# One plan for four layers: norms, routing and experts of a sandwich kernel by batch row

## The chip, the cores and the metric

The kernel runs on one core of a Trainium2 chip, in one launch. The metric is device microseconds of that core, the median of three runs. TensorE is PE, VectorE DVE, ScalarE ACT, GpSimd POOL; SyncE (SP) issues every DMA of the part that matters here.

## What is computed

`x` is (2, 1024, 128): two batch rows. A first block (layernorm, 16-head attention with cluster affinities, MLP) is added to it and is untouched by the change. The second block is `x + layernorm(ffn(layernorm(x)))`, all in float32, where `ffn` is four layers of

```python
h = _rms(x, ln1_w[l])
h = _attention(h, wq[l], wk[l], wv[l], wo[l], cos, sin, causal_bias)
x = jnp.clip(res + h, -100.0, 100.0)
...
h = _rms(x, ln2_w[l])
h = _moe(h, wr[l], wg[l], wu[l], wd[l])
x = jnp.clip(res + h, -100.0, 100.0)
```

with 16 query heads on 4 key heads of 64, causal, rotary; and 8 experts of width 256, of which the two likeliest count, `out += comb[e] * ((silu(x @ wg[e]) * (x @ wu[e])) @ wd[e])`. Every expert is computed for every token.

## The kernel before

Precision comes from split operands: each float32 matmul operand is a high part (a cast copy) and a low part (the difference), and a product is three matmuls, high by high, low by high, high by low. The high parts are made by ACT, the low ones by DVE or POOL.

A layer is one pass of a loop (`Fori`) that all five engines run. Four stages follow one another.

1. **Norm** (`norm_vector`, `norm_scalar`, `norm_tensor`, n5): 16 tiles of 128 tokens, both batch rows in one go: squares, sums, square root, scaling (L533), transposes (L584), then `xh` and `xl`.
2. **Attention** (`attention_order`, table `LAYER`): a "head" n is one key head with its four query heads, for one batch row: row n % 2, so heads 6 and 7 are the last of row 0 and row 1. Per head: projections P (three per half of the row), rotary products on DVE (L1483, L1484), halves swapped by DMA into `rbp`, sum on POOL (L771), high parts H on ACT, low parts L on POOL (L776) and K on DVE (L1489), copies Q by DMA into the stacks, maxima M (PE L1166, DVE L1501), turned into a row J and sent to the stack by DMA; then per step of 128 keys S (scores, L1184), exponential on ACT (L905), probabilities summed on POOL (L764), V (L1196), and per tile D (denominator L1208, reciprocal L1459) and O (L1215, L1472). The engines' order is computed ahead of time by `planned` from a cost in ns for each step and is fixed; head n+1 is prepared while head n attends, the first head while nothing does. W are the value projections of both rows.
3. **Norm n6 and routing**: again both rows at once; router matmuls (L1248, L1249), 19 dependent DVE steps (`route`, L1525 to L1545), then the weights of the experts turned into `combT` (8 partitions by 2048 tokens).
4. **Experts**: two experts per loop pass, both batch rows for one expert: a unit is 512 tokens by 128 of the hidden width. `up2` makes gate and up (six matmuls), ACT applies Silu (L933), DVE multiplies, POOL makes the low part (L788), `down2` adds three matmuls into one of four banks. The routing weight of a token reaches all partitions by a matmul of `sel` with `combT` into `psC`, and DVE multiplies by it:

```python
vec.tensor_tensor(hid[:, i % 4, :], gate[:, i % 2, :], psG[:, (2 * i + 1) % 3, :], ALU.mult).then_inc(s_hf, 1)
...
vec.tensor_tensor(hid[:, i % 4, :], hid[:, i % 4, :], psC, ALU.mult).then_inc(s_hc, 1)
```

Expert weights are loaded by SP into `est`, copied high on ACT (`split_high`, L879) and made low on POOL (`ready`, L744), once per expert.

## Time and profile before

| | |
|---|---|
| median of three runs | 3838.05 us (3833.82 to 3839.37) |
| profiled execution, its own time | 3821.54 us |
| its span | 3819.2 us |
| mean granted TensorE clock | 0.924 |
| busy: PE, DVE, ACT, POOL | 3384.5, 2759.9, 1672.0, 2031.2 us |
| share of the chain that ended last: PE, DVE, issue, POOL | 66%, 14%, 9%, 6% |

Durations below are of the profiled execution. A busy PE is not a PE at its peak: matmuls overlap, so the spacing of their starts says more than their durations.

### The profile page before, as it was taken

The page shows a single profiled execution, that of the slowest core. Times are in us where ns is not written, and L with a number is a line of the kernel's source. Part 1 is how long each engine was busy: PE and PEld are TensorE (multiplying, and loading weights), DVE is VectorE, ACT ScalarE, POOL GpSimd, SP SyncE. Part 2 cuts the span into 40 slices and gives each one's busy share as a digit, 9 for nine tenths or more (in the row PEclk, how much of TensorE's full clock was granted, in tenths as well). Part 3 has the DMA queues.
Part 4 walks back from the last instruction along what each step waited for, and adds up shares of the span by engine and source line. Part 5 has one row for each costly group of instructions (what it writes and reads, how often), then busy time and mean ns, then how long its engine had stood idle before and what let it go on. Part 6 is the DMA issues. An engine that isn't in the chain of part 4 may idle for free.

```text
span 3819.2 us, 65097 instructions
## 1 busy us (share of the span) xinstructions
PE 3384.5 (89%) x18456; PEld 2247.9 (59%) x18456; DVE 2759.9 (72%) x4711; ACT 1672.0 (44%) x3133; POOL 2031.2 (53%) x1615
## 2 busy tenths in 40 slices
PE   5899999739999979699999795999998869999897
PEld 2455555426666657466666574666656646666575
DVE  7877787358788756588886566887856668888566
ACT  3266666423444345334443453344334524444344
POOL 2100000036878646368787463778774638787654
PEclk9589899959999989799999897999998979999999
DMA  0000000043324101333331013333310134232001
GB/s 15 1 1 2 2 1 1 17 104 75 85 68 91 28 6 39 76 74 81 76 76 26 9 36 80 84 67 84 70 24 13 37 83 92 61 90 68 9 17 30
DMA packets 113175, 181.33 MB, mean 47 GB/s; under 512 B 26560, under 2 KB 54080, under 8 KB 112576
## 3 DMA queue, kind: packets, MB, share of 16 engines
q1 hardware_dynamic: 112832, 177.26, 20.1%
q8 instruction: 154, 2.52, 0.3%
q14 instruction: 189, 1.55, 0.1%
HBM read 23.45 MB, written 2.10 MB: 7 GB/s over the span
## 4 chain that ended last, share of the span: by engine, by line
PE 66%; DVE 14%; issue 9%; POOL 6%; ACT 3%; DMA 1%; SPq 1%; POOLq 0%; DVEq 0%; ACTq 0%
PE psO L1196 11%; PE psA L1184 7%; PE psA L1166 6%; PE psA L1185 6%; DVE rden L1459 4%; PE psO L1052 3%; PE psA L1040 3%; PE psA L1029 3%; PE psA L1272 3%; POOL xw L764 3%; PE psA L1274 3%; PE psA L1273 3%; PE psO L1215 2%; PE psO L1208 2%; PE psA L1169 1%
## 5 line engine op out<-in xcount | busy, mean ns | idle before, releaser
L905 ACT ACTIVATE prob<-psA 128x512 f32<-128x512 f32 x1152 | 658.4, 597 | 1083.7 <-PE psA L1185 321.9
L764 POOL TENSOR_TENSOR xw<-xw,prob 128x512 f32<-128x512 f32 x672 | 882.4, 1313 | 180.1 <-ACT prob L905 100.0
L1501 DVE TENSOR_REDUCE mxp<-psA 128x1 f32<-128x512 f32 (+3 forms) x1024 | 542.5, 583 | 129.4 <-PE psA L1166 118.8
L1184 PE MATMUL psA<-qs,ks 128*128 128x512 f32 x1152 | 539.0, 468 | 26.3 <-DMA qs<-mrow 21.9
L1459 DVE RECIPROCAL rden<-psO 128x256 f32<-128x256 f32 x256 | 449.2, 1755 | 153.5 <-PE psO L1208 116.9
L1166 PE MATMUL psA<-ks,qs 128*128 128x512 f32 (+3 forms) x1536 | 496.2, 399 | 50.7 <-DMA qs<-normed 49.0
L788 POOL TENSOR_TENSOR hidl<-hid,hidh 128x512 fp32r<-128x512 f32 x256 | 330.8, 1298 | 284.7 <-ACT hidh L943 284.5
L764 POOL TENSOR_TENSOR xw<-prob 128x512 f32<-128x512 f32 x224 | 291.7, 1302 | 353.3 <-ACT prob L905 265.7
L1185 PE MATMUL psA<-qs,ks 128*128 128x512 f32 x1152 | 455.4, 395 | 0.0
L1166 PEld LDWEIGHTS psA<-ks,qs 128*128 128x128 f32 x1536 | 299.9, 202 | 101.9 <-issue 53.7
L1400 DVE TENSOR_REDUCE mxp<-psA 128x1 f32<-128x512 f32 x512 | 315.2, 682 | 40.4 <-PE psA L1029 40.4
L853 ACT ACTIVATE pr<-psA 128x512 f32<-128x512 f32 x512 | 271.8, 602 | 125.6 <-PE psA L1040 124.3
L771 POOL TENSOR_TENSOR ra<-ra,rbp 128x512 f32<-128x512 f32 x192 | 240.1, 1281 | 145.9 <-DMA rbp<-rb 145.9
L1558 DVE TENSOR_TENSOR hid<-gate,psA 128x512 f32<-128x512 f32 x256 | 176.0, 687 | 189.6 <-ACT gate L933 189.5
L1184 PEld LDWEIGHTS psA<-qs,ks 128*128 128x128 f32 x1152 | 222.2, 193 | 144.9 <-issue 101.4
L1196 PE MATMUL psO<-prob,vv 128*64 128x256 f32 x2304 | 291.5, 385 | 3.1 <-ACT prob L905 2.9
L1196 PE MATMUL psO<-prob,outer 128*64 128x256 f32 x2304 | 291.4, 386 | 0.6
L933 ACT ACTIVATE gate<-psA 128x512 f32<-128x512 f32 x256 | 153.0, 598 | 251.1 <-PE psA L1274 250.9
L714 POOL COPY outer<-qkv 128x256 f32 x8 | 3.2, 402 | 465.1 <-PE psO L1052 465.1
L1501 DVE TENSOR_REDUCE mxq<-psA 128x1 f32<-128x384 f32 (+3 forms) x512 | 220.2, 483 | 35.8 <-PE psA L1169 31.2
L1169 PE MATMUL psA<-maskq,identb 128*128 128x128 bf16 x1024 | 241.9, 237 | 0.0
L1185 PEld LDWEIGHTS psA<-qs,ks 128*128 128x128 f32 x1152 | 220.4, 191 | 17.5
(244 smaller groups left out, 6454.3 us busy)
## 6 DMA issues: line engine op xcount, KB each, us to landing
qs<-normed SPq DMA_DIRECT2D x384, 256.0 KB, 4.9
rbp<-rb SPq DMA_DIRECT2D x256, 192.0 KB, 3.5
est<-in_L_ffn_wg SPq DMA_DIRECT2D x32, 128.0 KB, 2.1
est<-in_L_ffn_wu SPq DMA_DIRECT2D x32, 128.0 KB, 2.1
est<-in_L_ffn_wd SPq DMA_DIRECT2D x64, 64.0 KB, 1.9
wst<-in_L_ffn_wq SPq DMA_DIRECT2D x4, 512.0 KB, 4.4
wos<-in_L_ffn_wo SPq DMA_DIRECT2D x64, 32.0 KB, 2.1
outer_kept<-outer SPq DMA_DIRECT2D x1, 1024.0 KB, 6.4
```

The lines of the kernel that those rows point to most:

```text
L764: g.tensor_tensor(psum_k[:, t % 2, :], before, prob[:, i % 4, :], ALU.add).then_inc(s_su, 1 if kt > 1 else 2 + (t == 1))
L788: g.tensor_tensor(hidl[:, i % 4, :], hid[:, i % 4, :], hidh[:, i % 4, :], ALU.subtract).then_inc(s_hl, 1)
L853: act(pr1[:, j % 2, h, :], psS1[:, n % 3, :], ACT.Exp).then_inc(s_ex1, 1)
L905: act(prob[:, k % 4, :], psS[:, k % 2, :], ACT.Exp, scale=float(HD) ** -0.5).then_inc(s_ex, 1)
L1166: ins = mm(bank[:, 0:k1 - k0], qs1[b][:, c, h, t % TPC * P:(t % TPC + 1) * P], ks[b][:, 0, k0:k1], start=True, stop=not diagonal)
L1169: ins = mm(bank[:, k1 - k0 - P:k1 - k0], identb[:, :], maskq[:, :], start=False, stop=True)
L1184: mm(psS[:, i % 2, :], ks[b][:, 0, tile], qs1[b][:, c, :, qs], start=True, stop=False)
L1185: ins = mm(psS[:, i % 2, :], ks[b][:, 1, tile], qs2[b][:, c, :, qs], start=False, stop=(kt < t))
L1196: ins = mm(psO[t % 2][q * HD:(q + 1) * HD, 0:256], vv[b][:, kt, g * HD:(g + 1) * HD], prob[:, i % 4, q * 256:(q + 1) * 256], start=(kt == ...
L1400: vec.tensor_reduce(mxp1[:, m // 2, m % 2:m % 2 + 1], psM1[:, (m + 1) % 3, :], AX.X, ALU.max).then_inc(s_mr1, 1)
L1459: vec.reciprocal(rden[:, :], psO[t % 2][:, 256:512]).then_inc(s_rd, 1)
L1501: vec.tensor_reduce(dst, ring[SLOT["M", n, t, m] % N_RING][:, 0:k1 - k0], AX.X, ALU.max).then_inc(s_mr, 1)
```

## The change

The loop over layers goes: `network_order` plans the 4 layers as one table `NETWORK`, and each engine walks through it once, unrolled. In it

- norms are per batch row (steps Nc, Ns, Nv, Nd, Nm, T, Nh, Nl; q numbers them, four a layer), and so are routing (G, Ga, Ge, Gb, Gt, Gc) and experts: the order of units is row, expert, half of the row, half of the width, and each expert's weights are loaded and split once for each row (`Ew`, `Eh`, `El`), from two `est`;
- head 0's preparation in the next layer (`EARLY`) uses banks 6 and 7, which row 1's experts don't, and may run beside them; so may row 0's norm. Gate and up have banks 0 to 3, row 0's down sums 6 and 7, row 1's 4 and 5;
- routing weights are copied to `wrow`, written to DRAM (`Gd`), and come back by a DMA per 512 tokens that repeats them on all partitions (`B`, tile `spread`, three buffers); DVE multiplies by that tile. `combT`, `sel`, `psC`, `zeros` and their matmuls are gone. The hidden tile stays in `gate` (three buffers), and `hidh` and `hidl` have three;
- the gain of a norm is applied by the scale of ACT's copy and inside DVE's low part; the query's low part is written straight into its stack.

```diff
-def ring_order():
-    order = [("P", 0, c, u) for c in range(NCH) for u in range(3)]
-    for n in range(HEADS):
-        for c in range(NCH):
-            order += [("M", n, t, m) for t in range(c * TPC, (c + 1) * TPC) for m in range(len(max_pieces(t)))]
-            order += [("J", n, c)]
-            if n + 1 < HEADS:
-                order += [("P", n + 1, c, u) for u in range(3)]
-    return order
...
+EARLY = projections(0, 0) + [("W", j) for j in range(TPB // 2)] + projections(0, 1) + chunk_maxima(0, 0) + [("J", 0, 0)]
+MAIN = chunk_maxima(0, 1) + [("J", 0, 1)] + projections(1, 0) + [("W", j) for j in range(TPB // 2, TPB)] + projections(1, 1)
+for head in range(1, HEADS):
+    for half in range(NCH):
+        MAIN += chunk_maxima(head, half) + [("J", head, half)] + (projections(head + 1, half) if head + 1 < HEADS else [])
+N_PAIR = MAIN.index(("J", 0, 1)) + 1
+BANK = {item: 6 + i % 2 for i, item in enumerate(EARLY)}
+BANK.update({item: 2 + i % 2 if i < N_PAIR else (4, 5, 2, 3)[(i - N_PAIR) % 4] for i, item in enumerate(MAIN)})
+BEFORE, seen_in = {}, {}
+for item in EARLY + MAIN:
...
+UNITS = B * E * 4
+EXPERTS = L * B * E
+NORMS = 4 * L
...
+def unit(n):
+    return n // UNITS, n // (UNITS // B) % B, n // 4 % E, n // 2 % 2, n % 2
...
-def attention_order():
...
+def network_order():
...
+    def norm(q, b, ready, old, banks):
+        for h in range(2):
+            stage("scalar", ("Ns", q, h), 560, ready, ("tensor", ("T", q - 1, 1)) if q else None)
+        stage("vector", ("Nv", q), 1560, ("scalar", ("Ns", q, 1)))
+        stage("scalar", ("Nd", q), 1500, ("vector", ("Nv", q)))
+        stage("vector", ("Nm", q), 1700, ("scalar", ("Nd", q)))
+        for h in range(2):
+            stage("tensor", ("T", q, h), 500, ("vector", ("Nm", q)), *banks[h])
+            stage("scalar", ("Nh", q, h), 650, ("tensor", ("T", q, h)), *old)
...
+    def expert_weights(w):
+        l = w // (B * E)
+        stage("sync", ("Ew", w), 2000, ("gpsimd", ("El", w - 2)) if w > 1 else None,
+              ("tensor", ("S", l, HEADS - 1, TPB - 1, TPB - 1)) if w % (B * E) == 1 else None)
+        stage("land", ("Ew", w), 2500, ("sync", ("Ew", w)))
+        stage("scalar", ("Eh", w), 950, ("land", ("Ew", w)), ("tensor", ("Y", 4 * w - 5)) if w > 1 else None,
+              ("tensor", ("S", l, HEADS - 1, TPB - 1, TPB - 1)) if w % (B * E) == 1 else None)
...
+    def expert_unit(n):
+        l, b, e, c, f = unit(n)
+        w, k, g = n // 4, n // 2, B * l + b
+        start = [("scalar", ("S", l, HEADS - 1, TPB - 1, TPB - 1)), ("scalar", ("J", l, HEADS - 1, 1))] if n % UNITS < 2 else \
+            [("scalar", ("Si", n - 2)), ("vector", ("Hf", n - 2))]
+        if f == 0:
+            stage("sync", ("B", k), 650, ("land", ("Gd", g)), ("vector", ("Hw", 2 * k - 5)) if k > 2 else None)
+            stage("land", ("B", k), 2500, ("sync", ("B", k)))
+        stage("tensor", ("U", n), 1300, ("gpsimd", ("El", w)), ("vector", ("Nl", 4 * l + 2 + b, c)), *start)
+        stage("scalar", ("Si", n), 610, ("tensor", ("U", n)), ("gpsimd", ("Hl", n - 3)) if n > 2 else None)
+        stage("vector", ("Hf", n), 700, ("scalar", ("Si", n)))
+        stage("vector", ("Hw", n), 700, ("vector", ("Hf", n)), ("land", ("B", k)))
+        stage("scalar", ("Hh", n), 630, ("vector", ("Hw", n)), ("tensor", ("Y", n - 3)) if n > 2 else None)
+        stage("gpsimd", ("Hl", n), 1320, ("scalar", ("Hh", n)))
+        bank = [("vector", ("O", l, HEADS - 1, TPB - 1))] if b == 0 else [("scalar", ("Gc", g, 1))]
+        stage("tensor", ("Y", n), 650, ("gpsimd", ("Hl", n)), *(bank if e == 0 and f == 0 else []))
+    for l in range(L):
+        if l == 0:
...
+        for w in range(l * B * E, (l + 1) * B * E):
+            expert_weights(w)
+        if l + 1 < L:
+            weights(l + 1)
+        for n in range(l * UNITS, (l + 1) * UNITS):
+            expert_unit(n)
...
+NETWORK = network_order()
...
+        qs2_1, hidh, hidl, est1 = over("qs2_1", [P, NCH, GQ, CH], F32R, ("hidh", [P, 3, 512], F32R), ("hidl", [P, 3, 512], F32R), ("est1", [P, WE], F32))
...
+        est = [sb("est0", [P, WE], where=second), est1]
+        spread = sb("spread", [P, 3, 512], where=second)
...
+        qs1_1, eh1, el1, gate = over("qs1_1", [P, NCH, GQ, CH], F32R, ("eh1", [P, WE], F32R), ("el1", [P, WE], F32R), ("gate", [P, 3, 512], F32))
...
+        routing = nc.dram_tensor("routing_weights", (L * B, E, SEQ), F32, kind="Internal").ap()
...
+                elif what == "Gd":
+                    g = i[0]
+                    sp.wait_ge(s_cth, 2 * g + 2)
+                    sp.dma_start(routing[g], wrow[:, :]).then_inc(s_gd, 16)
+                elif what == "B":
+                    k = i[0]
+                    l, b, e, c, _ = unit(2 * k)
+                    sp.wait_ge(s_gd, 16 * (B * l + b + 1))
+                    if k > 2:
+                        sp.wait_ge(s_hw, 2 * (k - 2))
+                    sp.dma_start(spread[:, k % 3, :], routing[B * l + b, e:e + 1, c * CH:(c + 1) * CH].broadcast_to([P, CH])).then_inc(s_wb[k % 3], 16)
+                else:
...
-                nothing = zeros[:, :].unsqueeze(1).broadcast_to([P, NT, P])
-                g.tensor_tensor(combT[:, :].rearrange("p (a n) -> p a n", a=NT), nothing, nothing, ALU.add).then_inc(s_cz, 1)
...
+                    g_.wait_ge(s_hi, 4 * u + w + 1)
+                    if l and n == 1:
+                        g_.wait_ge(s_yd, UNITS * l)
+                        if w == 0:
+                            g.memset(qs2[1][0:HD, c, 0:GQ:2, :].bitcast(F32), 0.0).then_inc(s_qz, 1)
...
+                    g.tensor_tensor(hidl[:, n % 3, :], gate[:, n % 3, :], hidh[:, n % 3, :], ALU.subtract).then_inc(s_hl, 1)
...
+                    act(xh[:, b * SEQ + h * CH:b * SEQ + (h + 1) * CH], turned_bank(q, h), ACT.Copy,
+                        scale=fcol[:, w * L + l:w * L + l + 1]).then_inc(s_nh, 1)
...
-                def weights(ep, i):
-                    pair, i = l * (E // 2) + ep + i // (2 * N_UNIT), i % (2 * N_UNIT)
-                    ee, c = i // N_UNIT, i // 2 % 4
-                    if c == 0:
-                        t_.wait_ge(s_se, pair * 2 + ee + 1)
-                    t_.wait_ge(s_hc, pair * 2 * N_UNIT + i + 1)
-                    mm(psC, sel[:, ee, :], combT[:, c * 512:(c + 1) * 512], start=True, stop=True).then_inc(s_cb, 1)
...
-                for c in range(4):
-                    for n in range(4):
-                        ins = nc.tensor.transpose(acc[c][0:E, n * P:(n + 1) * P], comb[:, 4 * c + n, :], ident[:, :])
...
+                if n % UNITS < 2:
+                    t_.wait_ge(s_ex, (l + 1) * N_ATTN + 4)
+                    t_.wait_ge(s_mc, (l + 1) * HEADS * NCH)
+                else:
+                    t_.wait_ge(s_si, n - 1)
+                    t_.wait_ge(s_hf, n - 1)
+                expand(banks[2 * n % 4], n // 4, f * P, cs)
+                expand(banks[(2 * n + 1) % 4], n // 4, FF + f * P, cs).then_inc(s_gu, 1)
...
-                        vec.tensor_tensor(hid[:, i % 4, :], gate[:, i % 2, :], psG[:, (2 * i + 1) % 3, :], ALU.mult).then_inc(s_hf, 1)
-                        v.wait_ge(s_hf, n + 3)
-                        v.wait_ge(s_cb, (l * (E // 2) + ep) * N_UNIT + i // 2 + 1)
-                        vec.tensor_tensor(hid[:, i % 4, :], hid[:, i % 4, :], psC, ALU.mult).then_inc(s_hc, 1)
...
+                elif what == "Hf":
+                    n = i[0]
+                    v.wait_ge(s_si, n + 1)
+                    vec.tensor_tensor(gate[:, n % 3, :], gate[:, n % 3, :], banks[(2 * n + 1) % 4], ALU.mult).then_inc(s_hf, 1)
+                elif what == "Hw":
+                    n = i[0]
+                    v.wait_ge(s_hf, n + 1)
+                    v.wait_ge(s_wb[n // 2 % 3], 16 * (n // 6 + 1))
+                    vec.tensor_tensor(gate[:, n % 3, :], gate[:, n % 3, :], spread[:, n // 2 % 3, :], ALU.mult).then_inc(s_hw, 1)
...
```

DVE inside the experts. Before, a unit is two multiplications, the second with the weights in `psA`:

```order
L1558 TENSOR_TENSOR hid<-gate,psA 128x512
L1560 ISA
L1561 TENSOR_TENSOR hid<-hid,psA 128x512
L1555 REGISTER_ALU
L1556 REGISTER_ALU
L1558 TENSOR_TENSOR hid<-gate,psA 128x512
L1561 TENSOR_TENSOR hid<-hid,psA 128x512
```

Now, in the first layer's row 0 (`rt` and `r` are row 1's routing, `spread` the routing weights of row 0):

```order
L1758 TENSOR_TENSOR gate<-gate,psA 128x512
L1763 TENSOR_TENSOR gate<-gate,spread 128x512
L1640 TENSOR_REDUCE rt<-psA 128x64
L1642 TENSOR_REDUCE r<-rt 128x8
L1644 TENSOR_TENSOR rt<-rt,r 128x64
L1684 TENSOR_TENSOR wal<-wst,wah 128x1536
L1685 TENSOR_TENSOR wvl<-wvst,wvh 128x256
L1686 TENSOR_TENSOR wrp<-wrs,wrp 128x8
L1646 TENSOR_REDUCE r<-rt 128x8
L1648 TENSOR_TENSOR rt<-rt,r 128x64
L1650 TENSOR_TENSOR rt<-rt,order 128x64
L1652 TENSOR_REDUCE r<-rt 128x8
```

The second multiplication reads two tiles in SBUF, and the steps of row 1's routing, of which the rest follow without a break, stand between two units.

PE at the end of the experts. Before, the last units of a layer end it, and the next layer begins with the norm's transposes:

```order
L1288 REGISTER_ALU
L1289 MATMUL psA<-hidh,eh 128x512
L1290 MATMUL psA<-hidh,el 128x512
L1291 MATMUL psA<-hidl,eh 128x512
L1325 MATMUL psA<-ident,hid 128x128 x16
```

Now, among the last units of row 1 (`hidh`, `eh`: down and up of the first layer's experts; `ks`, `qs_0`: maxima of the second layer's head 0, `maskq` their mask):

```order
L1324 MATMUL psO<-ks,qs_0 128x128
L1327 MATMUL psO<-maskq,identb 128x128
L1324 MATMUL psO<-ks,qs_0 128x128
L1327 MATMUL psO<-maskq,identb 128x128
L1414 MATMUL psA<-hidh,eh 128x512
L1415 MATMUL psA<-hidh,el 128x512
L1416 MATMUL psA<-hidl,eh 128x512
L1324 MATMUL psO<-ks,qs_0 128x128
L1327 MATMUL psO<-maskq,identb 128x128
L1386 MATMUL psA<-xh,eh 128x512
L1387 MATMUL psA<-xl,eh 128x512
```

The maxima of the next layer's head 0, which stood behind the loop's end, now stand between units; its norm and projections stand further ahead among them in the same way.

## Rows read from the trace of the kernel before

**Rows 1.** Windows: us, then busy us of each engine (x instructions), PEclk, DMA share, GB/s
```profile
0.00:787.00 787.00, 650.09 (x3016) 363.53 (x3016) 566.27 (x1126) 421.70 (x935) 54.43 (x75) 0.87 0.04 9
787.00:853.90 66.90, 26.92 (x125) 21.53 (x125) 33.58 (x57) 21.14 (x33) 16.02 (x12) 0.63 0.40 92
853.90:1365.40 511.50, 494.44 (x3044) 321.19 (x3044) 397.58 (x660) 200.53 (x359) 379.09 (x294) 0.98 0.29 65
1365.40:1399.20 33.80, 19.64 (x80) 15.62 (x80) 22.89 (x44) 12.18 (x19) 3.60 (x1) 0.57 0.00 1
1399.20:1540.40 141.20, 139.56 (x593) 110.51 (x594) 87.88 (x128) 75.73 (x133) 95.47 (x77) 1.00 0.11 30
1540.40:1605.40 65.00, 30.24 (x147) 23.55 (x145) 37.19 (x62) 23.32 (x37) 15.71 (x13) 0.69 0.39 87
3793.00:3819.20 26.20, 3.94 (x22) 2.53 (x22) 16.25 (x22) 6.16 (x11) 1.28 (x1) 0.65 0.14 40
```

**Rows 2.** Timeline of PE inside the experts: start us, us, what; matmuls nine apart
```profile
1411.26 0.40 PE L1272 MATMUL psA<-xh,eh 128*128 128x512 f32 x1
...
1413.36 0.39 PE L1272 MATMUL psA<-xh,eh 128*128 128x512 f32 x1
```

**Rows 3.** Lines by source: count, then duration ns min/median/max, first and last start us
```profile
L1561 DVE TENSOR_TENSOR hid<-hid,psA x256: 686/687/690, 1400.0 to 3791.7; 128x512 f32<-128x512 f32 x128
L788 POOL TENSOR_TENSOR hidl<-hid,hidh x256: 1265/1299/1314, 1401.5 to 3793.2; 128x512 fp32r<-128x512 f32 x128
L744 POOL TENSOR_TENSOR el<-est,eh x32: 1809/1859/1866, 796.9 to 3770.7; 128x768 fp32r<-128x768 f32 x32
L1489 DVE TENSOR_TENSOR ks<-ra,ks x64: 689/1126/1631, 830.0 to 3530.1; 64x512 fp32r<-64x512 f32 x64
L764 POOL TENSOR_TENSOR xw<-xw,prob x672: 1262/1283/1759, 869.5 to 3612.0; 128x512 f32<-128x512 f32 x168
L933 ACT ACTIVATE gate<-psA x256: 570/598/602, 1391.6 to 3790.4; 128x512 f32<-128x512 f32 x128
L933 ACT ACT_TABLE_LOAD  x4: 1283/1283/1283, 1390.2 to 3643.1; - x4
L943 ACT ACTIVATE hidh<-hid x256: 621/623/634, 1400.8 to 3792.5; 128x512 fp32r<-128x512 f32 x128
```

**Rows 4.** Timeline of POOL and DVE: the scalings of both norms, the first beside POOL
```profile
1370.16 3.60 POOL L780 TENSOR_TENSOR combT<-zeros 128x2048 fp32r<-128x2048 f32 x1 [9.76 <-DVE veps L527]
1370.78 5.33 DVE L533 TENSOR_TENSOR normed<-inner,rstd 128x512 f32<-128x512 f32 x4
1555.30 2.50 DVE L533 TENSOR_TENSOR normed<-inner,rstd 128x512 f32<-128x512 f32 x4
```

**Rows 5.** Chain of waits before the second layer's first score: start us, us, what
```profile
1600.40 4.86 DMA qs<-mrow
```

**Rows 6.** Chain of waits at the end of the first layer's attention
```profile
1360.45 1.15 PE psO L1208 x4
...
1365.15 0.30 DVE inner L1472
```

**Rows 7.** Router matmuls (timeline of PE), and first and last routing step (chain of waits)
```profile
1381.77 0.38 PE L1248 MATMUL psO<-wrp,xh 128*128 128x16 f32 x1 [2.92 <-DVE xl L544]
...
1388.41 0.36 PE L1249 MATMUL psO<-wrp,xl 128*128 128x16 f32 x1
...
1388.81 0.44 DVE rt L1525
...
1395.06 0.30 DVE comb L1545
```

**Rows 8.** Window in the cluster attention's first maxima, and matmuls of a first projection (timeline)
```profile
140.00:180.00 40.00, 38.31 (x65) 18.07 (x64) 38.55 (x65) 0.39 (x2) 0.00 (x0) 0.50 0.00 1
...
1564.40 0.63 PE L1141 MATMUL psA<-xh,wal 128*128 128x512 f32 x1
1564.83 0.63 PE L1142 MATMUL psA<-xl,wah 128*128 128x512 f32 x1
```

More of the change, by code:

```diff
@@ L188, in attention_order @@
-        stage("gpsimd", ("S", n, t, kt), 1390 * (kt > 0), ("scalar", ("S", n, t, kt)), back("gpsimd", "S", 1),
+            return (engine, (what, l, *divmod(T - k, TPB))) if T >= k else None
+        first = [("scalar", ("Si", UNITS * l - 1)), ("vector", ("Hf", UNITS * l - 1))] if l and g == 0 else []
+        values = [("scalar", ("W", l, 4 * (n % B) + 3))] if n < B else []
+        stage("tensor", ("S", l, n, t, kt), 440 + 100 * (kt == t), ("land", ("J", l, n, t // TPC)) if kt == 0 else None,
+              back("scalar", "S", 2), *first)
@@ L549, in norm_vector @@
                     whole(c, xT[:, c * 512:(c + 1) * 512])
-            if n.turned == "split":
-                whole(0, xw[:, 0, :])
-                whole(1, xw[:, 1, :])
-                for c in range(4):
-                    low(c)
-                    if c < 2:
-                        own()
-                        whole(c + 2, xw[:, c % 2, :])
         def norm_scalar(a, n, run=0, start=()):
@@ L1572, in _ @@
+            norm_vector(v, n7, start=((s_nc, clips(NORMS + 1)),))
             v.wait_ge(n7.vec, n7.steps_vec)
```

1297 lines of the change are left out of this document (714 added, 583 removed).

## The prediction

> **What bounds the kernel now.** I read the span in stages first (busy time by window), then the chain of waits at the seams between stages, then single instructions in order of time. The stages say where TensorE (PE) is idle. After 787 us of cluster attention, each layer has four: 511.5 us of attention with PE shown busy 494; 33.8 us of norm and routing with PE busy 19.6; 141.2 us of experts with PE busy 139.6 at a granted clock of 1.00; and 65.0 us between the last expert and the first score of the next layer, PE busy 30.2 at 0.69 [rows 1]. Four times this, less one seam, plus a start of 66.9 and a tail of 26.2, is the span. So attention and experts are bound by PE, and the two seams, 99 us of 751, by chains. The seam behind the experts ends in a wait of 4.86 us for the row of maxima to land [rows 5]. Before the other one, the last tile's denominator, reciprocal, projection and add run alone from 1360.45 to 1365.45 [rows 6].
>
> Within the experts a unit (gate, up and down for 512 tokens and half of FF) is nine matmuls, and two starts nine matmuls apart differ by 2.10 us [rows 2]. VectorE (DVE) does two multiplications of 0.687 per unit, GpSimd (POOL) one subtraction of 1.299 and per expert one of 1.859 [rows 3]: they have room, PE has not.
>
> **What the change takes away.** The seams stop being serial. Row 0's norm and routing run under the last head, which is row 1's; row 1's run under row 0's experts; row 0's next norm, projections, maxima and turned row run under row 1's experts, as PE's order shows. What remains of both seams is the PE work in them, and what it displaces. The `sel`-`combT` matmul, one per two units, goes: 32 of 0.233 us (spacing [rows 2]), 7.5 a layer.
>
> **What it adds, and the term that decides.** The second multiplication of a unit was `hid`, in SBUF, by `psC`, in PSUM. It becomes `gate` by `spread`, both in SBUF. Before, the 256 of them take 686 to 690 ns whatever POOL does beside them [rows 3]. The instructions with two SBUF inputs behave otherwise. Four scalings of `inner` by `rstd` take 2.50 us with POOL idle, and 5.33 where POOL's 3.60 us instruction that clears `combT` was running when they began: 2.98 us of it were left, and 2.98+2.50 is 5.48 [rows 4]. The low half of a key, 689 ns at best, has a median of 1126 and a maximum of 1631; and POOL's sum of probabilities, median 1283, has a maximum of 1759, which is 1283 and most of a 689 [rows 3]. So each of the two waits out the other whole. I therefore cost the new multiplication as time taken from POOL: a unit holds what the two share for 0.687+1.299.
> The Trainium skill, "SBUF — State Buffer", section "Who interferes with whom", states this as a rule: a VectorE instruction with two SBUF inputs and a GpSimd instruction that reads SBUF exclude each other for the whole instruction. By it the sum stays as it is; by the planner's table, which gives both engines their own time only (700 and 1320 ns), the result would be rival 1.
>
> Experts of one layer, interior: 64 units of 1.986 are 127.1. The weights of an expert are now loaded and split once per batch row, 16 times instead of 8: 16 × 1.859 = 29.7. Together 156.8, above PE's 64 × 2.10 = 134.4: the bound moves. On the same pair come, of head 0's preparation (two halves), six `ra` sums of 1.28 and four low parts of 1.29 (taken as the other POOL subtractions of 512 columns, rows 3), 12.8; two key low halves, 1.4; four norm scalings at 2.50/4, 2.5; the low parts of the next attention weights, 1792 columns at 2.50 per 2048, 2.2. Sum 175.7. Row 1's routing is a row of dependent DVE steps, 6.3 us before for both rows [rows 7]; the steps are floors rather than columns, DVE's order puts sixteen of them between two units, and nothing of the experts passes: 6. Sum 181.7. The last row of maxima lands 4.86 us after its issue [rows 5], and PE has three maxima pieces, about 1 us, to fill it: +4. **185.7**, where 33.8+141.2+65.0 = 240.0 stood. In the last layer there is no next head: 156.8+1.3+6 = **164.1**, where 175 stood.
> PE in an interior stage: 134.4, 16 router matmuls in 3.4 (32 took 6.85 at the low clock [rows 7]), 18 projections at 0.233, 4.2, half of the values, 2.8 (24 of 256 columns, half of 0.233 each), 16 maxima pieces, some 4, and 48 small transposes, some 5.5: 154.3. It is covered by the 181.7 and costs nothing; without that cover it is rival 1.
>
> Attention of one layer: 511.5, plus the other half of the values 2.8, plus row 0's router matmuls and transposes 5.2, less 5.0 for the last tile's chain, which units 0 to 2 now cover [rows 6]. Row 0's routing weights are turned on PE ahead of scores, and the DVE steps before that may each wait behind a POOL sum: some ten of them, of 1.283 at most, POOL busy three quarters of the time: +4. **518.5**, PE-bound as before.
> Start: one batch row's norm instead of two before the first projection; the passes over `inner` halve (one is 2.50 [rows 4]), so −5: 62. Tail 26.2, left as it is.
> ScalarE switches its table 11 times a layer instead of 6, at 1.283 each [rows 3], 6.4 us more, and splits eight more experts; it was busy 75.7 of 141 [rows 1], so this costs nothing unless it lies in a unit's chain (rival 2). The Trainium skill, "ScalarE: Activation LUTs", section "Table sets: the hidden batching unit", puts a switch at about 2.7 us; by it the five would be 13.5, still under cover; the trace's 1.283 is used.
> SP issues the broadcasts of routing weights, 32 a layer, and each waits for a multiplication five units back; issue and landing have some 10 us before their user, while the nearest load of this trace's size, the row of maxima behind other transfers, took 4.86 [rows 5]. No cost; if one took over 10 us, each would add its excess, up to 128 times. Unrolling adds no cost that a row shows: between nothing and a few us either way.
>
> Sum: 787.0+62+4 × 518.5+3 × 185.7+164.1+26.2 = 3670.4 against the span of 3819.2: −148.8. The profiled execution took 3821.5, the median of the runs is 3838.1, so I take the difference off the median: **3690 us** (3689.3), 3.9% less.
>
> **Rivals.**
> 1. *The shared access costs nothing; PE is the bound.* Experts 154.3+4 in the interior layers, 143 in the last, attention without the 4: 787+62+4 × 514.5+3 × 158.3+143+26.2 = 3551, so **3570**. For it: PE was the bound at 1.00 for 141 us [rows 1]. Against it: the 5.33, the 1631 and the 1759 [rows 3, 4]. 0.12.
> 2. *The chain of a unit is the bound.* `gate` has three buffers, and a unit holds one for Silu 0.598, two multiplications 0.687, copy 0.623, subtraction 1.299 [rows 3], with handovers about 4.5 us; waiting behind one of POOL's 1.299 and one 1.859 makes 7.6, over three units of 2.45. If the order, planned without these waits, meets them in every expert, a unit takes about 2.8: 64 × 0.35 = 22 more in each of four stages: **3780**. For it: DVE too nears its limit in row 1's half, since each of its two-input instructions also holds it while it waits. 0.22.
> 3. *Slower: the clock falls.* PE now waits in every unit. Before, where PE had to wait for a reduction after each matmul, the granted clock was 0.50 for 40 us (1.2 instead of 2.4 GHz) although the row shows PE busy 38.3, and matmuls of 512 columns then start 0.43 apart [rows 8]. A unit would take 9 × 0.43 = 3.87, a whole stage some 100 us more. With half the units so: 3690+200 = **3890**. It decides from 157/4 = 39 us a stage on, about two units in five. Against it: PE still works 2.10 of 2.45, far more than there. 0.06.
> 4. *The overlap is incomplete*: head 0's preparation, norm and all, took most of the 65.0 us seam [rows 1] and must fit into row 1's 32 units, 78 us; if DMAs queued behind broadcasts and waits on POOL make it 20 late in three layers: **3750**. 0.08.
>
> **How the numbers follow.** The forecast has 0.52, with 3640 to 3740 for itself. The range leaves out rivals 1 and 3: **3590 to 3800**. About 0.2% is what a measurement tells from no change. Faster by more: forecast, 1, 4 and nearly all of 2, 0.91; within it 0.02; slower, rival 3 and a bad case of 2, 0.07.
>
> **What would show it.** Right: between attention stages about 186 us with no stretch of idle PE; the multiplication by `spread` with a median near 1.1 us instead of 0.69, and POOL's `hidl` with a maximum near 1.9; units about 2.45 apart; clock at 0.95 or above. Rival 1: 2.10 apart. Rival 2: 2.8, with ScalarE's Silu waiting for POOL. Rival 3: clock under 0.8 in the experts. Rival 4: idle PE before the first score. I am wrong altogether if attention itself leaves 512 by more than 10 us.

## The result, and the profile after

The changed kernel takes 3845.85 us in the median of 20 runs (3827.21 to 3859.59), the kernel before 3834.64 on the same chips: a ratio of 1.0028, 95% interval 1.0016 to 1.0040. It is slower by about 0.3%, where 3690 us and a gain of 3.9% stood. The profiled execution took 3827.21 us, the fastest of the 20, for a span of 3825.2, 6.0 more than the span before. The stages of [rows 1], now (windows: us, busy us of PE, PEld, DVE, ACT, POOL with instructions, PEclk, DMA share, GB/s):

```profile
787.00:839.80 52.80, 25.15 (x97) 17.13 (x97) 32.91 (x56) 17.19 (x29) 16.50 (x14) 0.63 0.44 98
839.80:1403.00 563.20, 525.10 (x3129) 342.75 (x3130) 428.24 (x696) 216.92 (x381) 382.72 (x297) 0.95 0.24 57
1403.00:1585.40 182.40, 157.33 (x690) 118.79 (x688) 145.60 (x204) 111.50 (x182) 138.93 (x88) 0.97 0.37 102
1585.40:2150.10 564.70, 525.31 (x3139) 343.44 (x3139) 433.77 (x704) 218.37 (x384) 384.55 (x299) 0.95 0.24 57
3644.70:3801.00 156.30, 140.19 (x588) 105.37 (x588) 113.11 (x153) 92.17 (x152) 120.83 (x76) 0.99 0.29 87
3801.00:3825.20 24.20, 2.37 (x13) 1.32 (x11) 14.62 (x20) 5.05 (x8) 1.26 (x1) 0.59 0.15 43
```

From the last addition of an attention to the next first score there were 240.0 us; there are 182.4. The start lost 14.1, the last experts and the tail 20.4. Those are the gains, 14.1 + 170.9 (three interior stages) + 20.4 = 205. But attention, 511.5 before, takes 563.2, and 211 us more over the four layers: it ate them all. That the two sums nearly cancel is chance. Cut at the first score of heads 0, 1 and 2 and of the last head, first the changed kernel, then before:

```profile
839.80:935.20 95.40, 83.16 (x418) 52.11 (x418) 57.91 (x95) 28.41 (x51) 48.18 (x38) 0.83 0.23 53
935.20:1014.50 79.30, 72.74 (x412) 46.70 (x411) 64.89 (x109) 25.91 (x47) 51.87 (x42) 0.94 0.31 71
1014.50:1078.30 63.80, 62.20 (x392) 41.58 (x392) 54.26 (x91) 26.23 (x47) 49.88 (x39) 1.00 0.29 67
1330.60:1403.00 72.40, 63.87 (x372) 39.46 (x372) 42.18 (x65) 33.07 (x56) 43.03 (x34) 0.95 0.09 29
```

```profile
853.90:932.50 78.60, 73.36 (x400) 46.91 (x401) 62.44 (x108) 26.79 (x48) 49.98 (x40) 0.93 0.38 86
932.50:994.10 61.60, 60.85 (x389) 40.20 (x389) 51.21 (x86) 25.19 (x46) 49.92 (x39) 1.00 0.35 78
994.10:1057.50 63.40, 62.09 (x390) 40.79 (x390) 52.03 (x90) 25.66 (x46) 48.71 (x39) 1.00 0.34 76
1304.70:1365.40 60.70, 54.77 (x331) 31.68 (x329) 29.36 (x40) 20.93 (x38) 39.22 (x31) 0.96 0.01 1
```

Head 0 is 16.8 us longer, head 1 17.7, the last head 11.7, and heads 2 to 6 together 5.5 (316.1 against 310.6).

**Where head 0 stands.** Windows of 5 us in the second layer's head 0, changed kernel, and then the same place of before:

```profile
1605.00:1610.00 5.00, 3.21 (x22) 1.92 (x18) 3.64 (x6) 0.00 (x0) 0.00 (x0) 1.00 0.01 2
1610.00:1615.00 5.00, 3.67 (x9) 2.16 (x9) 3.46 (x7) 0.00 (x0) 0.00 (x0) 0.54 0.00 0
1615.00:1620.00 5.00, 4.07 (x10) 2.28 (x10) 3.73 (x8) 0.00 (x0) 0.00 (x0) 0.50 0.00 0
1625.00:1630.00 5.00, 4.30 (x19) 3.95 (x19) 0.73 (x2) 1.28 (x3) 0.00 (x0) 0.50 0.00 0
1645.00:1650.00 5.00, 0.60 (x4) 0.29 (x4) 3.39 (x4) 1.23 (x3) 4.86 (x5) 0.80 0.86 192
```

```profile
1628.00:1633.00 5.00, 3.13 (x16) 1.70 (x12) 4.97 (x9) 0.00 (x0) 0.00 (x0) 1.00 0.00 0
1633.00:1638.00 5.00, 4.08 (x11) 2.11 (x10) 5.00 (x10) 0.00 (x0) 0.00 (x0) 0.52 0.00 0
```

Up to 1625.6 these are the maxima of head 0's second half; projections follow. Before, DVE is full beside the maxima; now neither engine is, POOL and ACT do nothing, and the clock sinks to about half from 1610 to 1635, 25 us (0.54, then 0.50 to 0.57), instead of 10. The timeline shows why, changed kernel first:

```profile
1612.82 1.16 DVE L1625 TENSOR_REDUCE mxp<-psA 128x1 f32<-128x512 f32 x2 [0.56 <-PE psA L1324]
1613.57 1.15 PE L1324 MATMUL psA<-ks,qs 128*128 128x512 f32 x2 [0.33 <-DVE mxp L1625]
1614.40 1.16 DVE L1625 TENSOR_REDUCE mxp<-psA 128x1 f32<-128x512 f32 x2 [0.42 <-PE psA L1324]
1619.14 1.29 DVE L1625 TENSOR_REDUCE mxp<-psA 128x1 f32<-128x512 f32 x2 [0.42 <-PE psA L1324]
1624.87 0.69 DVE L1625 TENSOR_REDUCE mxp<-psA 128x1 f32<-128x512 f32 x1 [0.30 <-PE psA L1327]
```

```profile
1633.65 4.86 DVE L1501 TENSOR_REDUCE mxp<-psA 128x1 f32<-128x512 f32 x8
```

Two banks: PE and DVE wait for each other, a pair every 1.58 us, 0.79 a maximum. Not every maximum is of full size, so the last tile's eight, all of 512 columns, are the fair comparison: on four banks they take 4.86 us, 0.61 each; on two banks, from 1619.14 to 1625.56, 6.42 us, 0.80 each. Two things come together. A pair of a full maximum and one of 0.41 us took 0.93 us on four banks; on two it took 1.27 while the clock was still 1.00 (1608.39 to 1609.66), and 1.58 once the clock had sunk. So about half of what such a pair loses is the waiting itself, and the rest comes with the low clock.

The last window of 5 us above, with PE at 0.60, is the second hole, and its cause lies 12 us earlier (timeline of SP, POOL, DVE and PE):

```profile
1633.78 2.44 SPq L792 DMA_DIRECT2D rbp<-rab  x4
1637.88 1.31 POOL L889 TENSOR_TENSOR xw<-prob 128x512 f32<-128x512 f32 x1 [33.55 <-issue]
1640.58 3.77 POOL L895 TENSOR_TENSOR rab<-rab,rbp 128x512 f32<-128x512 f32 x3
1646.55 0.69 DVE L1612 TENSOR_TENSOR rab<-psA,sinT 128x512 f32<-128x512 f32 x1 [12.79 <-POOL qs L904]
1649.65 1.12 PE L1361 MATMUL psO<-prob,outer 128*64 128x256 f32 x4 [4.40 <-ACT prob L1039]
```

Head 1's first projections come behind all 32 maxima, so their swap of halves goes to the queue at 1633.78, after POOL has been idle for 33.55 us, and everything of head 1 that hangs on POOL then falls beside the scores. POOL does head 1's sums and low parts first (1640.58 to 1647.66), the sum of probabilities waits behind them, ACT waits for that, and PE stands still for 4.40 us at the end of the chain.

**The last head**, groups of PE in it (line, shapes, count, busy us, mean ns, idle before; the busy times of groups overlap):

```profile
L1386 PE MATMUL psA<-xh,eh 128*128 128x512 f32 x9 | 3.8, 425 | 0.0
L1387 PE MATMUL psA<-xl,eh 128*128 128x512 f32 x9 | 3.5, 394 | 0.0
L1388 PE MATMUL psA<-xh,el 128*128 128x512 f32 x8 | 3.2, 394 | 0.0
L1457 PE MATMUL psA<-wrp,xl 128*128 128x16 f32 x8 | 2.0, 276 | 0.0
L1456 PE MATMUL psA<-wrp,xh 128*128 128x16 f32 x8 | 1.9, 268 | 0.7 <-DVE xl L1720 0.7
L1465 PE MATMUL psA<-ident,comb 128*8 128x128 f32 x8 | 1.9, 412 | 3.4 <-DVE comb L1677 3.4
L1429 PE MATMUL psA<-ident,normed 128*128 128x128 f32 x8 | 1.3, 280 | 0.2 <-DVE normed L1713 0.2
```

The busy times overstate what a group costs, since matmuls overlap. By the spacing of their starts in the same trace, row 0's norm, router and turning take 4.7 us (7.1 by their durations) and the first expert products, units 0 to 3 and the start of 4, take 6.3 (10.5); 2.7 us of maxima (4.9) have left the head for the one before.

**The experts.** The answers to [rows 3], by source:

```profile
L1763 DVE TENSOR_TENSOR gate<-gate,spread x256: 677/810/2308, 1397.6 to 3799.8; 128x512 f32<-128x512 f32 x128
L1758 DVE TENSOR_TENSOR gate<-gate,psA x256: 672/687/691, 1396.9 to 3799.1; 128x512 f32<-128x512 f32 x128
L912 POOL TENSOR_TENSOR hidl<-gate,hidh x256: 1257/1728/1859, 1399.9 to 3801.6; 128x512 fp32r<-128x512 f32 x128
```

The multiplication by `spread` takes 1.006 us in the mean and POOL's subtraction 1.538, where 0.687 and 1.299 (medians) stood; the one with a PSUM operand keeps its 0.687.

### The profile page after: what moved, and what is told of

It is laid out like the page before. It is cut to its first block, busy times and chain, and to the rows that moved or that the text cites. A ratio compares the mean times of both kernels' runs of the same rounds, so it can differ in the third digit from the quotient of the medians.

```text
span 3825.2 us, 55821 instructions
## 1 busy us (share of the span) xinstructions
PE 3391.4 (89%) x18312; PEld 2215.2 (58%) x18312; DVE 2892.2 (76%) x4763; ACT 1741.6 (46%) x3194; POOL 2142.9 (56%) x1615
## 3 DMA queue, kind: packets, MB, share of 16 engines
q8 instruction: 149, 2.44, 0.3%
## 4 chain that ended last, share of the span: by engine, by line
PE 49%; DVE 14%; POOL 8%; issue 4%; ACT 2%; DMA 0%; SPq 0%; DVEq 0%; POOLq 0%; ACTq 0%
PE psO L1361 11%; PE psA L1324 7%; PE psA L1346 7%; PE psA L1347 6%; DVE rden L1599 4%; POOL hidl L912 4%; PE psO L1381 3%; PE psO L1374 3%; DVE mxp L1625 2%; PE psA L1327 1%; DVE gate L1763 1%; PE psA L1349 1%; POOL rab L895 1%; PE psA L1386 1%; POOL el L908 1%
## 5 line engine op out<-in xcount | busy, mean ns | idle before, releaser
L1346 PE MATMUL psA<-qs,ks 128*128 128x512 f32 x1152 | 527.1, 458 | 12.6 <-ACT prob L1039 8.6
L1324 PE MATMUL psA<-ks,qs 128*128 128x512 f32 (+2 forms) x1472 | 498.6, 414 | 22.2 <-DVE mxp L1625 19.1
L912 POOL TENSOR_TENSOR hidl<-gate,hidh 128x512 fp32r<-128x512 f32 x256 | 389.8, 1538 | 131.2 <-ACT hidh L1090 130.7
L1324 PEld LDWEIGHTS psA<-ks,qs 128*128 128x128 f32 x1472 | 289.5, 204 | 87.5 <-DVE mxp L1625 47.4
L1361 PE MATMUL psO<-prob,outer 128*64 128x256 f32 x2304 | 296.4, 392 | 17.7 <-ACT prob L1039 17.7
L1758 DVE TENSOR_TENSOR gate<-gate,psA 128x512 f32<-128x512 f32 x256 | 173.2, 684 | 147.8 <-ACT gate L1084 146.8
L895 POOL TENSOR_TENSOR rab<-rab,rbp 128x512 f32<-128x512 f32 x192 | 243.5, 1297 | 63.9 <-DMA rbp<-rab 63.9
L1763 DVE TENSOR_TENSOR gate<-gate,spread 128x512 f32<-128x512 f32 x256 | 254.4, 1006 | 5.7
L1612 DVE TENSOR_TENSOR rab<-psA,sinT 128x512 f32<-128x512 f32 x168 | 115.6, 688 | 169.1 <-PE psA L1299 109.8
L1386 PE MATMUL psA<-xh,eh 128*128 128x512 f32 x512 | 210.0, 410 | 35.0 <-POOL el L908 22.0
```

What stands on the lines that cost most here:

```text
L895: g.tensor_tensor(ra[:, w, :], ra[:, w, :], rbp[:, w, :], ALU.add).then_inc(s_ad, 1)
L912: g.tensor_tensor(hidl[:, n % 3, :], gate[:, n % 3, :], hidh[:, n % 3, :], ALU.subtract).then_inc(s_hl, 1)
L1324: ins = mm(bank[:, 0:k1 - k0], qs1[b][:, c, h, t % TPC * P:(t % TPC + 1) * P], ks[b][:, 0, k0:k1], start=True, stop=not diagonal)
L1346: mm(psS[:, i % 2, :], ks[b][:, 0, tile], qs1[b][:, c, :, qs], start=True, stop=False)
L1361: ins = mm(psO[t % 2][q * HD:(q + 1) * HD, 0:256], vv[b][:, kt, g * HD:(g + 1) * HD], prob[:, i % 4, q * 256:(q + 1) * 256], start=(kt == ...
L1763: vec.tensor_tensor(gate[:, n % 3, :], gate[:, n % 3, :], spread[:, n // 2 % 3, :], ALU.mult).then_inc(s_hw, 1)
```

## The experiments

The first layer of each profile, us: heads from first score to first score, the last head to its last addition, and from there to the next first score; then the time's ratio to before with its interval.

| run | head 0 | head 1 | heads 2–6 | last head | to next score | ratio |
|---|---|---|---|---|---|---|
| before | 78.6 | 61.6 | 310.6 | 60.7 | 240.0 | 1 |
| changed | 95.4 | 79.3 | 316.1 | 72.4 | 182.4 | 1.0028 [1.0016, 1.0040] |
| e_banks | 84.8 | 78.2 | 321.0 | 74.3 | 183.2 | 0.9924 [0.9907, 0.9940] |
| e_order | 96.4 | 68.9 | 316.1 | 70.8 | 182.3 | 0.9942 [0.9921, 0.9963] |
| e_both | 87.0 | 66.0 | 315.5 | 72.8 | 182.5 | 0.9829 [0.9807, 0.9852] |
| b_two | 86.6 | 61.6 | 310.7 | 60.2 | 241.1 | 1.0074 [1.0051, 1.0098] |
| b_late | 83.9 | 79.4 | 308.7 | 60.7 | 240.7 | 1.0202 [1.0161, 1.0244] |
| e_late | 95.9 | 77.8 | 316.1 | 59.8 | 209.7 | 1.0162 [1.0139, 1.0185] |
| e_gt | 94.8 | 80.3 | 316.1 | 72.0 | 181.6 | 1.0049 [1.0030, 1.0067] |
| e_psum | 96.6 | 80.5 | 316.1 | 72.8 | 167.6 | 0.9898 [0.9881, 0.9914] |
| e_all | 85.4 | 67.2 | 317.1 | 73.0 | 168.0 | 0.9677 [0.9648, 0.9706] |
| e_turn | 90.6 | 64.9 | 317.9 | 77.9 | 167.9 | 0.9714 [0.9670, 0.9758] |
| e_turnm | 87.9 | 65.2 | 323.5 | 77.2 | 174.3 | 0.9801 [0.9754, 0.9849] |
| e_turngt | 88.6 | 65.2 | 322.0 | 72.5 | 174.1 | 0.9778 [0.9735, 0.9822] |
| a_seq | 94.0 | 76.0 | 311.3 | 78.2 | 182.7 | 0.9990 [0.9976, 1.0004] |
| e_seq | 87.7 | 64.4 | 310.8 | 76.9 | 167.2 | 0.9617 [0.9600, 0.9634] |
| e_seq1 | 86.9 | 62.3 | 310.9 | 78.2 | 166.6 | 0.9586 [0.9565, 0.9607] |
| e_intseq | 83.6 | 65.3 | 310.9 | 76.7 | 167.3 | 0.9561 [0.9534, 0.9588] |

### Banks and projections, in the changed kernel

```diff
-N_PAIR = MAIN.index(("J", 0, 1)) + 1
+N_PAIR = 8
```

> The changed kernel, with the maxima of head 0's second half on four PSUM banks in turn from the ninth on, where the change keeps all 32 on two. Nothing else is edited. Changed kernel: about 3846 us; its head 0 takes 95 to 98 us from first score to first score, its head 1 79. T1 (the two banks make each maximum wait for the reading of the one before last): head 0 comes down by 10 to 17 us in each layer, and the time to 3780 to 3806. T2 (what costs is that head 1's projections come behind all of head 0's maxima): head 0 gains 4 us at most, head 1 stays at 79, the time stays above 3830. Rival (attention is longer because the clock is lower or because of DMA traffic everywhere): no change in heads 0 and 1.

3805.69 us. Head 0 falls by 10.6 to 14.2 us in the four layers, head 1 by 1.1 to 3.6: T1 holds. Heads 2 to 6 grew by 4.9 in the first layer, which no theory had (below: with the same banks and another order, `e_seq` has 310.8).

```diff
-MAIN = chunk_maxima(0, 1) + [("J", 0, 1)] + projections(1, 0) + ...
+MAIN = chunk_maxima(0, 1)[:8] + projections(1, 0) + chunk_maxima(0, 1)[8:] + [("J", 0, 1)] + ...
```

> The changed kernel, with head 1's first three projections moved ahead in the turn of the banks, behind the first eight maxima of head 0's second half instead of behind all 32. The maxima stay on two banks. T1 (two banks): head 0 stays at 95 to 98 us, the time above 3830. T2 (late projections): head 1 falls from 79 us to 62 to 66 and the time by 4 x 13 to 4 x 17 us, to 3778 to 3794; head 0 may lose 2 to 4 us of this, since three projections of 1.3 us lie ahead of its maxima. Rival (clock or DMA): no change in either head.

3812.30 us, above T2's 3778 to 3794: the late projections do cost, but at less than T2's price. Head 1 comes to 68.9, not to 62 to 66, and head 0, which T2 let fall by 2 to 4, grows by 1.0 to 3.4 in the four layers.

> Both edits: four banks from the ninth maximum of head 0's second half on, and head 1's first projections behind the first eight of them. If T1 and T2 each hold for one head: head 0 about 80 us, head 1 about 63, so 4 x 33 us less, about 3714 us. If only one of them holds, the time is that of the run with it alone (3780 to 3806). If both are one and the same starved stretch, told twice: less than the sum of the two runs, 3740 to 3780. Rival: no change.

3764.73 us. The number lies in the range given for one stretch told twice, but its reason does not hold: each edit alone gave 1.04 and 0.86% of the time of before, both 1.99%, so they add up. Head 0 comes to 87.0 and head 1 to 66.0, not to 80 and 63, and they keep 8.4 and 4.4 us over before.

### The same two things alone, in the kernel before

In `b_two` the ring's bank of head 0's maxima from tile 4 on is their index modulo 2 instead of 4. In `b_late` the order of the ring is changed for head 0 alone:

```diff
-            if n + 1 < HEADS:
-                order += [("P", n + 1, c, u) for u in range(3)]
+            if n + 1 < HEADS and (n or c):
+                order += [("P", n + 1, h, u) for h in (range(NCH) if n == 0 else [c]) for u in range(3)]
```

> The kernel before (about 3834 us), with one thing of the change alone: the 32 maxima of head 0's second half take their turns on two PSUM banks of the ring instead of four. T1: head 0 goes from 78.7 us to 86 to 95 in each layer, the time up by 30 to 65 us, to 3864 to 3899. Rival (the two banks cost only together with what the change moved into head 0, the second row's normalisation and half of the projections of the values): under 3 us a layer, under 3846.

3864.98 us. Head 0 goes to 86.6, +8.0, at a granted clock of 0.88 where 0.93 stood; every other head stays within 0.6:

```profile
868.40:955.00 86.60, 77.93 (x400) 48.59 (x401) 63.74 (x109) 26.57 (x48) 50.70 (x40) 0.88 0.35 78
```

Nearly all of the 8.0 stands in the maxima themselves: from the first reduction of the 32 to the end of the last DVE needs 26.8 us before (860.56 to 887.32) and 34.5 here (874.58 to 909.11). In the changed kernel it is 34.9, in `e_banks` 28.5.

> The kernel before, with the other thing alone: head 1's first three projections take their turns behind all maxima of head 0 instead of ahead of those of its second half; four banks stay. T2: head 1 goes from 61.6 us to 70 to 78, head 0 keeps its 78.7 or gains 2 of them (the projections leave it), so 3834 + 4 x 7 to 4 x 16 = 3862 to 3898. Rival (head 1 has enough cover in before, so that late projections are taken up by its scores): under 3846.

3921.58 us, above the whole expected range. Head 1 shows the changed kernel's length with 79.4, but head 0 grows too, by 5.3, where none or a gain was expected:

```profile
872.70:956.60 83.90, 75.11 (x389) 45.23 (x389) 54.41 (x92) 25.88 (x46) 47.07 (x37) 0.91 0.28 62
956.60:1036.00 79.40, 72.35 (x410) 46.84 (x409) 64.03 (x111) 26.95 (x48) 51.98 (x42) 0.96 0.37 86
```

The growth of head 0 is not in the maxima, whose stretch is even 0.9 us shorter (25.8), but behind them. Head 0 from the end of its last maximum on, before and here:

```profile
887.30:932.50 45.20, 44.67 (x256) 29.89 (x257) 35.36 (x64) 18.73 (x34) 35.86 (x29) 0.96 0.47 106
```

```profile
905.70:956.60 50.90, 46.16 (x245) 28.11 (x245) 28.68 (x48) 20.12 (x36) 39.31 (x31) 0.90 0.46 102
```

Head 1's first three sums and two low parts, which POOL did at 861.8 to 868.1 before, now stand at 918.5 to 924.7 beside the scores. PE waits 2.54 us for an exponential behind them, and the next 5 us have a clock of 0.50. This is the second hole of the changed kernel. Head 1 is longer because work has moved into it: 54 of DVE's maxima lie in it instead of 30, and 35 instead of 57 in head 0, which got no shorter for losing them.

So in the first layer the late projections cost 23.1 us and the two banks 8.0, without anything else of the change. Neither has to do with overlap, unrolling or traffic.

### Row 0 in the last head

```diff
-        stage("vector", ("Nc", q), 650, ("vector", ("O", l, HEADS - B + b, TPB - 1)))
+        stage("vector", ("Nc", q), 650, ("vector", ("O", l, HEADS - 1, TPB - 1)))
```

> The changed kernel, with row 0's clipping, and so its normalisation and routing behind it, only after the last addition of the last head of a layer instead of beside that head. T3 (the last head is longer by 12 us because of the idle waits and the work of row 0 in it: 5 us of TensorE's work and 7 of waits): last head back to 60 to 62 us from its first score to the last addition (72.4 in the changed kernel), and the time from that addition to the first expert product about 20 to 25 us instead of none, so 4 x (+8 to +14) = 3877 to 3900 us. Rival (the last head is longer for another reason, as wrong bank turns or lower clock all over): it stays at 70 or more, and the time rises by 4 x 20, to 3925.

3898.57 us; the last head takes 59.8. The run takes row 0's norm and routing out of it and with them the first expert products, which hang on them, so its 12.6 us come with the three together and not with norm and routing alone. The way to the next score grows by 27.3 against 12.6 won: the overlap is worth about 15 us a layer, though nearly half of it is paid back. The first expert product followed after 7.0 us, not 20 to 25; the routing's delay shows later in the stage, where POOL stands still for 34.3 us until its first hidden tile, at 1429.0.

```diff
-        stage("vector", ("Gb", g), 3600, ...
+        stage("vector", ("Gb", g), 9000, ...
```

> The changed kernel, with the planner's cost of the longer part of a row's routing on VectorE at 9.0 us (it took 7.6 us in the last head) instead of 3.6, which moves the turning of row 0's routing weights on TensorE behind three more score tiles. T3a (TensorE's standstill of 3.4 us in front of that turning is what the last head pays beyond its work): last head 72.4 to about 69, 4 x 3 us less, the time 3834. Rival (the standstill only moves to another place of a head whose scores wait for the reciprocals and divisions queued on VectorE): within 4 us of 3846.

3850.04 us: T3a falls in this plan. In the first layer the standstill in front of the turning shrinks from 3.4 to 0.6 us and the last head is still 72.0; in the other layers it is 1.8 to 3.4 us longer than in the changed kernel.

### The experts

```diff
-gate = gate * banks[up]
-gate = gate * spread
+banks[up] = banks[up] * spread
+gate = gate * banks[up]
```

> The changed kernel, with the two multiplications of an expert unit on VectorE in another order: first the up bank in PSUM by the spread weights, back into PSUM, then the gate by that bank. The count of VectorE instructions, their size and what they wait for are the same, but neither reads two tiles of SBUF any more; the up bank comes free one instruction later. T4 (VectorE's instructions that read two tiles of SBUF and GpSimd's shut each other out, and this sets the pace of the experts, 182.5 us a layer): the multiplication by the spread weights falls from a mean of 1.0 us to about 0.7, GpSimd's low part from a mean of 1.54 to under 1.35, the experts to 158 to 170 us a layer and 140 to 148 the last, the time by 50 to 90 us, to 3756 to 3796. Rival (PE bounds the experts, or the chain of a unit): durations may fall, the experts stay within 5 us a layer and the time above 3825.

3794.11 us, in the range of T4. 167.6, 167.8 and 173.3 us in the interior stages, the last of them over T4's 158 to 170, and 140.5 in the last layer's. Lines of the profile, busy us and mean ns behind the bar:

```profile
L1763 DVE TENSOR_TENSOR psA<-psA,spread 128x512 f32<-128x512 f32 x256 | 178.5, 697 | 169.4 <-ACT gate L1084 168.7
L1758 DVE TENSOR_TENSOR gate<-gate,psA 128x512 f32<-128x512 f32 x256 | 175.8, 687 | 8.5
L912 POOL TENSOR_TENSOR hidl<-gate,hidh 128x512 fp32r<-128x512 f32 x256 | 339.2, 1332 | 141.4 <-ACT hidh L1090 137.6
```

As many instructions of the same size, and 15 us of a stage are gone (9 in the third), with each at nearly its undisturbed length: the shared access set the pace of the experts, and a PSUM operand in each multiplication avoids it. The Trainium skill, "SBUF — State Buffer", section "Who interferes with whom", has the exclusion as a rule; the trace agrees (the second multiplication falls from 1.006 to 0.697 us, POOL's subtraction from 1.538 to 1.332).

> The changed kernel with the three edits that each won: four banks, head 1's projections ahead, and the multiplications of an expert unit through PSUM. If they are independent (attention against experts): the 1.71% of the first two and the 1.3% that the third gained against the changed kernel add up, 3835 x 0.983 - 51 = 3719 us, 3705 to 3730. If the experts' gain rests on room that the two others use up: 3740 or more.

3713.40 us: the three are independent, and the version beats both kernels by over 3%.

### Why the middle heads are longer

> The changed kernel with the three winning edits, and a rule of the planner of before put back: on TensorE, projections, maxima and turnings of the row of maxima keep the one order of their banks' turns, where the change orders them by kind. T5 (the middle heads, 64.6 us here against 62.7 before, lose by the order that the planner finds, since TensorE idles 2.3 us of a head behind the exponentials): middle heads 62.5 to 63.5, 3713 - 4 x 5 x 1.5 = 3683, 3670 to 3695. Rival (they lose by bank turns, DMA traffic or the clock): still 64 or more, 3705 to 3720.

> As the run with the old rule, and with the planner's costs of before for the maxima (0.08 us less each), the low part of the keys (0.7 us), the last maxima and the two DMA issues. The plan then repeats itself from head to head as that of before does. T5: middle heads 62.5 to 63, so 3675 to 3690. Rival: no better than the changed kernel's 63.5, 3690 to 3715.

> As the run before it, with the cost of the routing at 9.0 us too. If T3a holds, 8 to 14 us under that run; if the standstill only moves, within 4 us of it.

3728.78, 3758.84 and 3743.63 us, the first two above even their rivals' ranges. T5 in this form falls: the old rule gave middle heads of 63.8 and 64.7 us in turn, the old costs with it 65.0, where 64.6 was to be mended. The third is 15 us under the second, where T3a said 8 to 14. The intervals of the two ratios overlap, but in the profiles PE's standstill of 3.3 us in front of the turning is gone and the last head is 3.3 to 4.7 us shorter in all four layers. So T3a, which fell in the changed kernel's plan, is likely to hold in this one: what a cost in the planner is worth depends on the plan around it. Plans that give 63.5, 64.6 and 65.0 us a head for the same scores and maxima pointed at the order as such. So the next runs gave the planner, as added dependencies, before's own order of every engine from the first score of head 2 to that of head 7:

```diff
+            for name, after in zip(names[1:], names):
+                plan[engine, name][1].append((engine, after))
```

> The changed kernel with the same instructions, but from the first score of head 2 to the first score of head 7 every engine works in the order that the plan of before has for these heads. T6 (the order alone makes the middle heads longer): 63.5 us a head back to 62.7, 4 x 5 x 0.8 = 16 us less, 3825 to 3835. Rival (the DMAs, the code of four layers written out, the bank turns): 63.5 stays, 3842 or more.

3827.59 us: 62.7 a middle head, as before, with the bank turns, the DMAs and the unrolled code of the change; T6 holds for these heads. The same head of the second layer in this run and in the changed kernel:

```profile
1834.60:1897.30 62.70, 61.71 (x391) 40.92 (x390) 51.86 (x89) 25.87 (x46) 49.08 (x39) 1.00 0.30 68
```

```profile
1889.50:1953.10 63.60, 61.31 (x390) 41.09 (x390) 53.51 (x88) 26.21 (x47) 48.99 (x39) 1.00 0.29 67
```

PE works as long in both; only its idle time differs, 1.0 and 2.3 us. The last head gives 5.8 back in the first layer (3.2 in the second), since before's order leaves more of its maxima to it (4.5 us of their matmuls there, 0.8 in the changed kernel), so attention as a whole is 2.4 to 3.6 us a layer shorter. Over the four layers heads 2 to 6 win 20 us, the last head takes 16 of them back, and head 1, whose order was not set, wins 9. That the time fell by about T6's 16 us is therefore in part luck: in this kernel before's order of the middle heads moves work more than it saves time.

> The changed kernel with the three winning edits (3713 us, middle heads 64.6 us) and before's order for heads 2 to 6. T6: 62.7 us a head, 4 x 5 x 1.9 = 38 us less, 3670 to 3685. Rival: no change, 3705 to 3720.

3686.95 us, 2 over the range. Here the order pays more than it costs: heads 2 to 6 win 31 us over the four layers against `e_all`, and the last head gives 14 back.

> As that run, with head 1 in before's order too (67.3 us without it, 61.6 before). T6: head 1 at 62 to 65 and up to 4 x 5 us below that run, but head 0 may give part of it back, since more of head 1's maxima then have to be done before head 1's first score: 3660 to 3685. Rival: no gain over that run.

3669.86 us, head 1 at 62.3.

> As the run before, with the projections of the values of row 1 laid between the maxima of head 0's second half instead of behind them. If TensorE's idle time beside these maxima is what is left of head 0's 86 us: the four projections (1.3 us each) fill it, 4 x 3 to 4 x 5 us less, 3645 to 3670. Rival (VectorE sets the pace there, and each projection in between makes it wait): no gain, or some us more.

3667.37 us. Head 0 gains 3.3 to 4.3, head 1 loses 3 of them: within the intervals no gain over the run before. Both are the best here, 4.1 to 4.4% under before.

## Why the prediction was wrong

**The step that failed** is the one that begins "Attention of one layer: 511.5" and ends "518.5, PE-bound as before". It took the heads over whole and added only the work that moves in. The runs price the first layer's +51.7 us as follows: two banks 8.0 (`b_two`), late projections 23.1 (`b_late`), row 0 in the last head 12.6 (`e_late`), together 43.7. The first two prices are taken in the kernel before. Undone in the changed kernel (`e_both`, where the projections come behind eight maxima and not ahead of all), the same two things gave back 21.7 of these 31.1, and 12.8 us of heads 0 and 1 stayed.

The other 8.0 us are open. Of them 3.4 are in head 0 and were not tested apart; the values' projections, put at 2.8, are now in it. The last 4.6 are in heads 2 to 7 (371.3 before, 388.5 in the changed kernel, 375.9 in `e_late`). The planner's order makes heads 2 to 6 longer, as `a_seq` shows, but with before's order heads 2 to 7 together take 389.5, so that the order costs these 4.6 is not shown. "PE-bound as before" was false for the 16 us in which head 0's maxima alternate between PE and DVE, and in the hole where PE waits 4.40 us for a chain through POOL.

The causes in heads 0 and 1 both stood in the diff: one line gives the items before `N_PAIR` two banks, the line above it puts `projections(1, 0)` behind `chunk_maxima(0, 1)`. The low clock beside such maxima stood in [rows 8], 0.50 for 40 us, but the price did not: its 65 maxima in 40 us are 0.62 each, close to what four banks give here. I used that row for rival 3, and placed it in the experts, where each stage kept 0.97 and more. A part of rival 3's mechanism did come, in head 0: PE waits, and its clock is 0.83 where 0.93 stood. The largest term, the late projections, was in no rival, and the slower side had a chance of 0.07.

**Row 0 in the last head** was put at 5.2 of work plus 4 of waiting less 5 of a covered chain, 4.2; it is 12.6. The work was right: norm, router and turning take 4.7 us of PE. The products of units 0 to 3 and the start of 4, 6.3 us, were counted as cover for the last tile's chain and not as length. They covered nothing in sum: PE idles 8.5 us in this head, 7.5 in `e_late` and 5.9 in the kernel before. These 6.3 us are missing from the experts' stage in turn.

**The experts.** 185.7 was forecast and 182.4, 183.1 and 182.7 came; the last stage 164.1 against 156.3. Both are a little flattered, since 6.3 us of products lie ahead of the stage, of which I had counted 5. That the two engines wait each other out is shown by `e_psum`. The signs: in row 0's half, starts of units are 2.44 us apart in the mean, as forecast (2.45), if one gap of 11.5 us is left out in which row 1's routing stands; in row 1's half, with head 0's preparation in it, 2.87, and without it, in the last layer, 2.44. The median of the multiplication is 0.81, not 1.1, with a mean of 1.006; the maximum of `hidl` 1.859, as said; the clock 0.97 and 0.99. Rival 1, with its 158.3 a stage, is what `e_psum` comes near (167.6), not what the change does. Rival 2 did not come: the mean over the interior stage is its 2.8, but from the work of head 0 in between, and ACT's Silu waits for POOL for only 3.4 us of the first layer's stage. Rival 4 gave 20 us a layer for three layers in case the overlap was incomplete, and placed them before the first score; there PE has two short holes, 1.95 and 1.40 us, in the last 5.4.

**The start** was put at 62 and took 52.8, **the tail** at 26.2 and took 24.2. The broadcasts of `spread` land after 3.2 us in the median, well within the 10 allowed.

The sum, redone with what was measured (means over the layers for attention and the interior stages): 787.0 + 52.8 + 4 × 564.2 + 3 × 182.7 + 156.3 + 24.2 = 3825.2. Of the difference to 3670.4, 4 × 45.7 = 183 is attention, and the other terms give 28 back.
